# A selective scan's drive: dt*u*B made by ScalarE with tokens on partitions and transposed by TensorE, instead of a product with a diagonal of B

## What is computed

```
dA  = exp(dt[..., None] * A)
dBu = (dt * u)[..., None] * Bm[:, :, None, :]
h   = dA_t * h + dBu_t          # over the tokens t, for each d and n
y   = einsum('bld n, bln -> bld', hs, Cm) + u * D
```

## Time and profile before

| what | value |
|---|---|
| runs | 1469.52, 1472.12, 1475.14 us; median 1472.12 |
| the profiled execution | 1469.62 us, of it 1467.7 us from first to last instruction |
| PE busy | 1243.6 us (85%), weight loads 752.8 us |
| DVE busy | 1057.6 us (72%) |
| ACT busy | 856.1 us (58%) |
| POOL busy | 409.5 us (28%) |
| mean granted TensorE clock | 0.934 of full speed |
| costliest PE line | L1426, the drive: 2048 instructions, 274.1 us |
| its counterpart on ACT | L701, the diagonals: 512 instructions, 162.4 us |

### The profile page before, as it was taken

The page is one execution under the profiler, slowest core; times in us unless marked ns, Lnnn a source line. Parts: engine busy times, 40 slices in busy tenths (PEclk is TensorE's granted clock), DMA queues, the critical chain, the costliest instruction groups (busy, mean ns, idle before and its releaser), DMA issues. The chain is left out here.

```text
span 1467.7 us, 19284 instructions
## 1 busy us (share of the span) xinstructions
PE 1243.6 (85%) x6505; PEld 752.8 (51%) x6505; DVE 1057.6 (72%) x1671; ACT 856.1 (58%) x1781; POOL 409.5 (28%) x348
## 2 busy tenths in 40 slices
PE   3886889898999989898999989898899989876874
PEld 1343346553665446653656446554656446534643
DVE  0755558877886888967886878967886887855644
ACT  2542677567664767657573766657574766436531
POOL 2010005420354005420254005430254004422541
PEclk9986899999999999999999999999999999986995
DMA  2000001100110002100010001101010002101110
GB/s 69 1 8 0 1 30 59 36 1 30 29 56 17 31 1 58 44 1 30 23 57 23 18 13 58 44 1 30 22 51 22 30 1 58 37 0 44 51 29 7
DMA packets 31409, 41.24 MB, mean 28 GB/s; under 512 B 4617, under 2 KB 14674, under 8 KB 31314
## 3 DMA queue, kind: packets, MB, share of 16 engines
q1 hardware_dynamic: 31314, 40.02, 9.0%
HBM read 37.65 MB, written 2.36 MB: 27 GB/s over the span
## 5 line engine op out<-in xcount | busy, mean ns | idle before, releaser
L608 POOL TENSOR_TENSOR read<-state,c_row 128x1024 f32<-128x1024 f32 x128 | 301.6, 2363 | 338.3 <-DVE state L1118 85.1
L1118 DVE TENSOR_TENSOR_SCAN state<-decay,bank 128x512 f32<-128x512 f32 x256 | 298.7, 1205 | 88.1 <-PE bank L1426 81.9
L1426 PE MATMUL bank<-diagonal,dtu_t 128*128 128x128 f32 x2048 | 274.1, 288 | 55.4 <-DVE state L1118 51.4
L1426 PEld LDWEIGHTS bank<-diagonal,dtu_t 128*128 128x128 f32 x2048 | 256.9, 199 | 99.6 <-issue 85.8
L1442 PE MATMUL bank<-read,ident 128*128 128x512 f32 x512 | 244.4, 606 | 0.0
L690 ACT ACTIVATE decay<-dt,neg_a 128x510 f32<-128x510 f32 x256 | 169.5, 711 | 71.9 <-DVE state L1118 71.8
L701 ACT ACTIVATE diagonal<-ident,b_t 128x128 f32<-128x128 f32 x512 | 162.4, 390 | 29.1 <-PE bank L1426 29.1
L1366 PE MATMUL bank<-znt,omega 128*128 128x512 f32 x256 | 144.2, 646 | 29.4 <-ACT sqf L681 29.4
L1128 DVE TENSOR_TENSOR s_sb<-bank,causal 128x512 f32<-128x512 f32 x128 | 87.8, 686 | 80.0 <-PE bank L1379 80.0
L1442 PEld LDWEIGHTS bank<-read,ident 128*128 128x128 f32 x512 | 93.7, 198 | 80.4 <-issue 78.9
L678 ACT ACTIVATE expf<-bank,minus_s,root2s 128x512 f32<-128x512 f32 x128 | 99.4, 777 | 60.3 <-PE bank L1366 59.2
(11 more groups left out here) (234 smaller groups left out, 1770.7 us busy)
## 6 DMA issues: line engine op xcount, KB each, us to landing
c_row<-c_rows SPq DMA_DIRECT2D x128, 256.0 KB, 3.2
xa<-x_dram SPq DMA_DIRECT2D x8, 256.0 KB, 3.6
out_dram<-x SPq DMA_DIRECT2D x8, 256.0 KB, 2.4
omega<-omega_t_dram SPq DMA_DIRECT2D x1, 512.0 KB
c_rows<-xdbl SPq DMA_DIRECT2D x8, 32.0 KB, 1.6
wqkv<-w_qkv_t_dram SPq DMA_DIRECT2D x1, 192.0 KB
state<-w_down_dram SPq DMA_DIRECT2D x1, 176.0 KB, 2.7
state<-w_gate_dram SPq DMA_DIRECT2D x1, 128.0 KB, 2.0
```

The costliest lines, as they stand in the source:

```text
L608: pool.tensor_tensor(read[:, s % STATE_BUFFERS], state[:, s % STATE_BUFFERS], c_row[:, s % C_BUFFERS].unsqueeze(1).broadcast_to([P, DT, TO ...
L1118: dve.tensor_tensor_scan(state[:, s % STATE_BUFFERS, c], decay[:, s % 2, c].rearrange("p b t -> p (b t)"), bank[:, DRIVE_BANK + c], 0.0, A ...
L1426: last = pe.matmul(bank[:, DRIVE_BANK + c, t * P:(t + 1) * P], dtu_t[:, t, c * P:(c + 1) * P], diagonal[:, s % DIAGONALS, t], start=True, ...
```

## The change

ACT multiplies `dtu_t` itself by B: for each token tile the 128x256 tile of dt*u (tokens on partitions) times the scale B[token, n] of each partition, into `by_token` (two buffers, as `diagonal` had). PE only transposes the result, eight 128x128 tiles a state, into the same banks. The wait for `dtu_t` moves from PE to ACT. Since the first products now need `dtu_t`, ACT makes states 0 and 1 at k=14 and 15 of loop B (before: 10 and 11), and PE's first drive stands at k=15 (before: 14). Waits on buffers, the other states' slots and all other work stay.

```diff
-DIAGONALS = 2
+DRIVES = 2
...
-        diagonal = sb("diagonal", [P, DIAGONALS, TILES, P])
+        by_token = sb("drive_by_token", [P, DRIVES, TILES, INNER])
...
-            def diagonal_in(gb, s):
+            def drive_by_token(gb, s):
 
                 act.wait_ge(b_t_done.sem, b_t_done.at(gb, 1))
-                act.wait_ge(drive_ps.sem, drive_ps.at(gb, max(s + 1 - DIAGONALS, 0) * DT))
+                act.wait_ge(dtu_t_done.sem, dtu_t_done.at(gb, DT))
+                act.wait_ge(drive_ps.sem, drive_ps.at(gb, max(s + 1 - DRIVES, 0) * DT))
                 for t in range(TILES):
-                    last = act.activation(diagonal[:, s % DIAGONALS, t], ident[:], ACT.Identity,
+                    last = act.activation(by_token[:, s % DRIVES, t], dtu_t[:, t], ACT.Identity,
                                           scale=b_t[:, t, s:s + 1])
-                last.then_inc(diagonal_done.sem, 1)
+                last.then_inc(by_token_done.sem, 1)
...
-                if turn.has_mid and k in (10, 11):
-                    diagonal_in(mid, k - 10)
+                if turn.has_mid and k in (14, 15):
+                    drive_by_token(mid, k - 14)
                 if turn.has_mid and k in (13, 14):
                     decay_in(mid, k - 13)
...
-                        diagonal_in(turn.old, k + 2)
+                        drive_by_token(turn.old, k + 2)
...
             def drive(gb, s):
 
-                pe.wait_ge(dtu_t_done.sem, dtu_t_done.at(gb, DT))
-                pe.wait_ge(diagonal_done.sem, diagonal_done.at(gb, s + 1))
+                pe.wait_ge(by_token_done.sem, by_token_done.at(gb, s + 1))
                 for c in range(DT):
                     scanned = half_done if c == 0 else state_done
                     pe.wait_ge(scanned.sem, scanned.at(gb, s))
                     for t in range(TILES):
-                        last = pe.matmul(bank[:, DRIVE_BANK + c, t * P:(t + 1) * P],
-                                         dtu_t[:, t, c * P:(c + 1) * P],
-                                         diagonal[:, s % DIAGONALS, t], start=True, stop=True)
+                        last = pe.transpose(bank[:, DRIVE_BANK + c, t * P:(t + 1) * P],
+                                            by_token[:, s % DRIVES, t, c * P:(c + 1) * P],
+                                            ident[:])
                     last.then_inc(drive_ps.sem, 1)
...
-                if turn.has_mid and k == 14:
+                if turn.has_mid and k == 15:
                     drive(mid, 0)
```

More of the change, by code:

```diff
@@ L370, in build @@
         dtu_t_done = events("b_dtu_t", DT)
-        diagonal_done = events("b_diagonal_of_b", STATES)
+        by_token_done = events("b_drive_by_token", STATES)
         dt_ps = events("b_dt_in_psum", DT)
```

## The result

The kernel after takes 1425.7 us (median of four runs, 1423.5 to 1428.2) against 1471.8 us for the kernel before on the same chip: a ratio of 0.969, with an interval of 0.967 to 0.971, or 46 us less. The profiled execution took 1427.11 us, 1425.2 us of it from first to last instruction; against the span before, 1467.7 us, that is 42.5 us less.

What follows compares the result with a forecast made beforehand. Loop A was taken to alternate between PE-bound and DVE-bound slots. Gains of 6.1, 26.0, 4.5 and 8 make 44.6 us, less 5.6 leaves 39: 1469.6 to 1430.6, called 1431 us; forecast 1418 to 1445, wider range 1410 to 1456.

Steps and rivals of the forecast that it cites:

- allowance for the clock: Longer PE gaps in DVE's slots bring more half-clock stretches: 0.8 us in each of seven turns, 5.6 us off the gain.
- turn 9: Last turn: state step from 3.50 to 2.82 us, set by ACT, saves 4 us; first half another 4; 8 in all.
- PE's part: Drive of eight transpositions takes 0.90 us instead of 1.79; PE loses 114 us of work over 128 drives.
- ACT's part: Four 256-column products take 1.60 us a state instead of 1.17: +0.43, 6.0 us in loop A, hidden wherever ACT waits anyway.
- ACT is what is late next: Loop A of turn 5, state 11: the tanh stands behind decay 12 and state 13's product, leaving 4.4 of 5.2 us gained.
- The move: First products and drive later in loop B cost nothing; `ctx_t` in time by 0.3 us; otherwise up to 1 us a turn.
- Loop A of turn 5: Shorter drives make scans 6, 11 and 15 earlier by 3.0, 5.2 and 5.8 us; the loop ends 6.1 us earlier.
- Rival 1: ACT's longer products delay decay, tanh and QKV copies: half the gain goes, 21 us, to 1452; chance 0.23.
- Rival 2: Transpositions keep PE at half clock at the head of loop A in some turns: slower, 1527 us; chance 0.06.
- Rival 3: A transposition of fresh data costs PE what a product does: time as before within a few us; chance 0.03.
- Rival 4: Full clock throughout and ACT hidden: gain of 49 to some 55 us, to 1415; chance 0.12.

Runs made afterwards that it cites:

- Kernel 3: Kernel after, but ACT multiplies only the first 128 columns and PE transposes these for both halves (output not the reference's): 1427.5 us, 0.9697 of the kernel before.
- kernel 6: Kernel after with the second tanh of FFN a put ahead of the product in ACT's queue in slot 11: 1427.6 us, 0.9688 of the kernel before.
- kernel 7: Kernel after with the edits of both kernel 5 and kernel 6: 1428.6 us, 0.9689 of the kernel before.
- kernel 10: Kernel after with PE's first drive back in slot 14 of loop B, ACT's products unchanged: 1451.3 us, 0.9833 of the kernel before.
- kernel 5: Kernel after with eight zero-tile products on PE in slots 6, 7, 11 and 12 of loop A, turns 2 to 7: 1428.6 us, 0.9688 of the kernel before.
- kernel 8: Kernel after with ACT's product of each state made as eight instructions of 128 columns: 1457.5 us, 0.9891 of the kernel before.
- kernel 4: Kernel after with each transposition done twice, 16 a drive: 1476.7 us, 1.0035 of the kernel before.
- kernel 2: Kernel after, but PE transposes by products with the identity, 16 instructions a drive: 1479.7 us, 1.007 of the kernel before.
- experiment 1: Kernel before with the move alone: diagonals 0 and 1 at slots 14 and 15 of loop B, first drive at 15; median 1477.6 us, ratio 0.9991.

## Why the prediction was right, point by point

**The time.** 1431 us forecast, 1425.7 measured, in the forecast's own range; the account predicted 39 us out of the span, and 42.5 came. Part of that closeness is luck, as the parts show. Ahead of the allowance for the clock, the forecast had 32.1 us for the loops A of turns 2 to 7, 4.5 for turn 8, 8 for turn 9 and nothing elsewhere; measured are 32.8, 4.1 (with loop B of turn 7), 5.5, another 2.3 in the loops B and -2.3 ahead of turn 2, and those two cancel. Within the 32.8, turn 5 gave 2.2 more than its 6.1 and the other five together 1.4 less than their 26.0.

**PE's part: right.** 0.90 us a drive was taken, 0.87 is there; 114 us in all, 112.7 measured. The Trainium skill's factor of four ("TensorE: Matmul & The Clock Gate", section Terms) was not there: eight tiles cost 1.79 us as products and 0.87 as transpositions, a factor of two.

**ACT's part: right in size, and it costs less than I thought.** The product takes 1.60 us a state as estimated between the rows of 128 and 510 columns, as the start of the next instruction on ACT shows, and the total is 54.6 us higher, where 0.43 x 128 is 55:

```profile
728.09 1.69 ACT L702 ACTIVATE drive_by_token<-dtu_t,b_t 128x256 f32<-128x256 f32 x4
729.68 1.04 ACT L762 ACTIVATE sqf<-qk 128x1024 f32<-128x1024 f32 x1
```

**The step "ACT is what is late next" named the right wait, but gave it a price that it doesn't have.** VectorE does wait for the tanh in slot 11, 0.79 us, and the prediction took 0.8 us of the gain off for it (4.4 of 5.2 left). But the kernel before waited there too, 0.60 us:

```profile
777.69 0.89 DVE L1033 SCALAR_TENSOR_TENSOR a_ffn_h<-a_ffn_h,bank 128x704 f32<-128x704 f32 x1 [0.60 <-ACT a_ffn_h L725]
```

So only 0.2 us was lost: scan 11 gained 5.95 us (counted from scan 0) and this step 5.8. That the 0.79 is near the 0.8 is chance. Kernel 3 halves the wait (0.4), kernels 6 and 7 too (0.3), and none is faster.

**The move: right.** At the end of loop B state 0's product ends 1.9 us behind the masked copy (2.0 forecast), and the context copy stands behind state 1's product, 0.7 us later than before (5.0 us behind the masked copy, before 4.2), where 1.2 was forecast:

```profile
696.86 0.38 ACT L711 ACTIVATE s_sb<-bank 128x256 f32<-128x256 f32 x1 [1.50 <-DVE s_sb L1129]
697.14 1.69 ACT L702 ACTIVATE drive_by_token<-dtu_t,b_t 128x256 f32<-128x256 f32 x4
698.74 1.32 ACT L690 ACTIVATE decay<-dt,neg_a 128x510 f32<-128x510 f32 x2
699.96 0.36 ACT L711 ACTIVATE s_sb<-bank 128x256 f32<-128x256 f32 x1
700.23 1.69 ACT L702 ACTIVATE drive_by_token<-dtu_t,b_t 128x256 f32<-128x256 f32 x4
701.82 0.58 ACT L719 ACTIVATE ctx_t<-bank 128x512 f32<-128x512 f32 x1
```

```profile
702.05 0.87 PE L1473 MATMUL bank<-ident,b_ffn_h 128*128 128x128 f32 x6 [0.65 <-DVE b_ffn_h L1088]
702.76 0.60 PE L1414 MATMUL bank<-ident,ctx_t 128*128 128x128 f32 x4
```

PE's wait for VectorE is 0.65 us instead of 1.30, so 0.65 us of cover was used, and `ctx_t` is still in time, by 0.4 us (ready at 702.4, used at 702.76; 0.3 forecast). Loop B of turn 5 kept its length. What the prediction didn't ask is what the products would do without the later drive: some 3 us a turn, by kernel 10.

**Loop A of turn 5: the mechanism right, the sizes small.** Counted from scan 0, the forecast gain of turn 5's scans 6, 11 and 15 was 3.0, 5.2 and 5.8 us; it is 3.6, 5.95 and 8.2. About 1.1 us of the difference arises at the head of the loop, where the kernel before had a stretch of low clock (718 to 722 us) and the kernel after has none. Predicted for VectorE's wait for drives was half of the 11.7 us, and 2.6 is left.

**The allowance for the clock: right in sign, and no saving is to be had by removing it.** I took 5.6 us off for more low stretches. They came: summed over windows of 1 us, the time at half clock is 226 us after and 192 before, and the loops A of turns 2 to 7 hold 14 stretches where they held 7. The price in loop A of the one that kernel 7 removes is 0.4 to 0.7 us a turn, somewhat under the 0.8 that was taken. None of kernels 5 to 7 earned the term back. The loops A came to 32.8 us with their stretches in, where the forecast with its allowance has 27.3 (32.1 less six times 0.8), so the shorter drives gave more than was worked out, and the allowance hid it; that the sum without it (44.6 us) is nearer to the 42.5 is luck again.

**Turn 9: the step that failed.** Forecast 8 us, 4 in each half, with a state step of 2.82 us set by ACT; measured 5.5 us, and the steps of the second half are set by PE:

```profile
1356.53 2.33 DVE L1119 TENSOR_TENSOR_SCAN state<-decay,bank 128x512 f32<-128x512 f32 x2 [2.47 <-PE bank L1426]
1359.13 2.33 DVE L1119 TENSOR_TENSOR_SCAN state<-decay,bank 128x512 f32<-128x512 f32 x2 [0.26 <-PE bank L1426]
1361.87 2.33 DVE L1119 TENSOR_TENSOR_SCAN state<-decay,bank 128x512 f32<-128x512 f32 x2 [0.41 <-PE bank L1426]
```

The scans are 2.60 and 2.74 us apart, and each waits for PE. ACT's own step is what I said, 2.83 us (decays at 1358.90, 1361.73 and 1364.55), but it starts ahead of PE, and no states are left for which the lead could run out. So the step is better than forecast, and still the second half (scan 9 to scan 15) gained 2.6 us and not 4: the sum of states ahead of the drive that the first of these scans waits for ran at the lower clock (3.52 us at 1352.44, elsewhere 1.88), which the forecast didn't count in this turn.

The first half, up to scan 9, gained 2.5 us. The sum passed over its start with "4", and at scan 3 nothing has been gained yet. PE's first drive, and the gates behind the second one, in the kernel before and in the kernel after:

```profile
1337.49 6.66 PE L1426 MATMUL bank<-diagonal,dtu_t 128*128 128x128 f32 x32 [1.45 <-ACT dtu_t L824]
1343.99 1.35 PE L1452 MATMUL bank<-wgate,b_ffn_xqt 128*128 128x352 f32 x4
```

```profile
1301.54 1.97 PE L1426 MATMUL bank<-ident,drive_by_token 128*128 128x128 f32 x8 [2.47 <-ACT drive_by_token L702]
...
1306.12 2.26 PE L1452 MATMUL bank<-wgate,b_ffn_xqt 128*128 128x352 f32 x4
```

There PE does wait for ACT, since the first product now stands behind the copies of `dtu_t`: 2.47 and 0.85 us for the two drives, where it waited 1.45 for both. Of what the shorter drives save, 0.9 us is left when the gates start, and the gates, which in this execution ran at the lower clock (2.26 us instead of 1.35), used it up. VectorE's step behind the tanh then comes just as long after dt*u as before (13.4 us).

**The rivals.** Rival 1 (ACT takes it back) is true of a heavier product: kernel 8 pays 30 to 32 us for 95. At the change's own size kernel 3 refutes it. Rival 2 (the clock stays down) is refuted by kernel 4 against kernel 2. Rival 3 (no saving on PE) is refuted by the 0.87 us. Rival 4, 1415, is not reached even with ScalarE's price gone (kernel 3) or four of the gaps filled (kernel 5). In turn 5's loop A VectorE is busy for 64.6 of 70.6 us, so at most 6 us are left there ahead of it; that a lighter VectorE would now shorten the loop is to be expected from this and was not tried.

## What to carry to other kernels

Work moved off a nearly full engine is worth only what the next fullest leaves: TensorE's drives lost 113 us and the kernel 46. In a loop A of 77 us VectorE's busy time was only 9.5 us behind TensorE's, and the loop gained 4 to 8. Price the added work on the receiving engine by trying it both lighter and heavier: here lighter brought nothing and heavier cost a third of the added work, and neither end shows in a sum of busy times. When an operand is now made later, move its first consumer behind the work that others wait for; that one slot was worth 21 to 26 us. And before a wait is charged to a change, look how long it was before: the tanh's 0.79 us had been 0.60.

## What the runs showed that was not expected

**One kernel, two times.** The kernel of experiment 1 ran in 1459.0 to 1463.9 us four times and in 1477.3 to 1481.7 six times on one chip. Its profiled execution was one of the four. A turn of it, and the same turn of the kernel before (columns as in the earlier trace rows):

```profile
716.30:880.10 163.80, 148.22 (x814) 90.62 (x813) 132.10 (x208) 106.41 (x222) 48.95 (x40) 0.98 0.10 30
```

```profile
722.46:889.04 166.58, 150.57 (x825) 92.91 (x824) 131.11 (x208) 106.17 (x222) 49.01 (x41) 0.97 0.09 29
```

In that execution each of turns 3 to 6 took 163.8 us, with two low stretches each, at the same two places of every turn (at 781 and 832 us, then at 945 and 996); the kernel before has its stretches in other places from turn to turn. No run of the six was profiled, but their mean granted clock is on record: 0.938 to 0.943 in the four, 0.927 to 0.932 in the six. By my estimate from these means (twice the shortfall of the clock from 1, times the span) the six spent some 35 us more at the lower clock, for 18 us more of time. So the low stretches do go with the two times; where they fell in the six, and what decides between the two, stays open. It does mean that the effect of a small edit in such a loop can't be read off one run: the two groups are 1.2% apart.

**Where a low stretch falls matters more than how many there are.** Kernel 7 has a stretch less in loop A and one more in loop B than the kernel after, and the same time; one in loop B cost 1.64 us, one in loop A 0.4 to 0.7. Kernel 6 has one stretch in loop B of turn 5 where the kernel after has two, and the loop is 1.4 us longer.
